# Waiting block by block in the dense down projection, and other places for two small pieces of work

## The reference

```python
x = x + 0.5 * L0_ffn(norm(x))   # stage 1, dense:   down(silu(gate) * up), 384 hidden
x = x + L0_attn(norm(x))        # stage 2, mixing:  a recurrence over time (WKV)
x = x + 0.5 * L0_ffn(norm(x))   # stage 3, dense:   same weights as stage 1
x = x + 0.5 * L1_ffn(norm(x))   # stage 4, experts: 8 experts, the best 2 per token
x = x + L1_attn(norm(x))        # stage 5, flow attention
x = x + 0.5 * L1_ffn(norm(x))   # stage 6, experts: same weights as stage 4
```

```python
gate = einsum('bsd,hd->bsh', x, w_gate / 127)
up   = einsum('bsd,hd->bsh', x, w_up / 127)
out  = einsum('bsh,dh->bsd', silu(gate) * up, w_down / 127)
```

## Time and profile before

| | |
|---|---|
| median of three runs | 1009.28 us |
| the profiled execution | 1007.76 us |
| its span (first to last instruction) | 1006.0 us |
| PE busy | 859.9 us (85%) |
| DVE busy | 711.1 us (71%) |
| ACT busy | 638.6 us (63%) |
| POOL busy | 604.4 us (60%) |
| mean granted clock of TensorE | 0.947 |

### The profile page before, as it was taken

How to read it: one execution, slowest core, us unless ns; L and a number is a source line. 1 busy time by engine, 2 the same in 40 slices (tenths; PEclk the granted TensorE clock), 3 DMA queues, 4 the chain that set the end, 5 groups by cost and what they waited for, 6 DMA issues and landing times.

```text
span 1006.0 us, 14102 instructions
## 1 busy us (share of the span) xinstructions
PE 859.9 (85%) x3862; PEld 460.3 (46%) x3862; DVE 711.1 (71%) x1535; ACT 638.6 (63%) x1153; POOL 604.4 (60%) x610
## 2 busy tenths in 40 slices
PE   7879677767975999999996688888886899999997
PEld 6734333354432444444443355555543344444443
DVE  6945469965563878887863277777786787887774
ACT  3167489967755887778783444444322787778884
POOL 2064675667458766666675254444457766667674
PEclk9999788869997999999997799999997999999999
DMA  8000000000002222211120000000000213223320
GB/s 213 11 1 0 0 0 1 1 1 1 1 0 85 84 86 85 79 48 58 69 84 0 1 1 0 1 1 1 1 1 1 101 69 95 94 94 95 94 95 22
DMA packets 27406, 42.10 MB, mean 42 GB/s; under 512 B 5320, under 2 KB 19036, under 8 KB 27356
## 3 DMA queue, kind: packets, MB, share of 16 engines
q1 hardware_dynamic: 27356, 41.52, 13.0%
HBM read 39.15 MB, written 2.36 MB: 41 GB/s over the span
## 4 chain that ended last, share of the span: by engine, by line
PE 35%; issue 22%; DVE 19%; POOL 14%; ACT 9%; SPq 1%; DVEq 0%; POOLq 0%; DMA 0%; ACTq 0%
PE bank L1478 7%; PE bank L1480 7%; PE bank L1479 7%; POOL arena L810 5%; POOL arena L754 4%; PE bank L1708 3%; DVE arena L1324 3%; ACT bank L1001 3%; POOL rstd L712 2%; DVE arena L1367 1%; DVE arena L1366 1%; DVE stats L1173 1%; PE bank L1678 1%; ACT arena L993 1%; PE bank L1715 1%
## 5 line engine op out<-in xcount | busy, mean ns | idle before, releaser
L790 POOL TENSOR_TENSOR arena<-arena 128x512 f16<-128x512 f32 x256 | 295.3, 1166 | 125.3 <-ACT arena L993 123.5
L1324 DVE TENSOR_TENSOR arena<-bank,arena 128x512 f32<-128x512 f32 x256 | 172.5, 685 | 79.6 <-ACT bank L1001 63.3
L993 ACT ACTIVATE arena<-arena 128x512 f16<-128x512 f32 x256 | 160.8, 628 | 73.8 <-DVE arena L1324 73.7
L1001 ACT ACTIVATE bank<-bank,eb 128x512 f32<-128x512 f32 x256 | 166.8, 656 | 18.9 <-PE bank L1480 18.5
L817 POOL TENSOR_TENSOR arena<-arena 128x512 f32<-128x512 f32 (+1 forms) x24 | 32.7, 1371 | 117.2 <-DVE arena L1442 89.9
L1478 PE MATMUL bank<-arena,ew1hi 128*128 128x512 f16 x256 | 98.5, 385 | 2.0 <-DVE arena L1324 2.0
L1479 PE MATMUL bank<-arena,ew1hi 128*128 128x512 f16 x256 | 98.5, 385 | 0.0
L1480 PE MATMUL bank<-arena,ew1lo 128*128 128x512 f16 x256 | 97.9, 382 | 0.0
L1478 PE MATMUL bank<-arena,ew2hi 128*128 128x512 f16 x256 | 97.3, 380 | 0.1
L1479 PE MATMUL bank<-arena,ew2hi 128*128 128x512 f16 x256 | 97.3, 380 | 0.0
L1480 PE MATMUL bank<-arena,ew2lo 128*128 128x512 f16 x256 | 97.3, 380 | 0.0
(11 more groups left out here) (274 smaller groups left out, 1876.2 us busy)
## 6 DMA issues: line engine op xcount, KB each, us to landing
arena<-wrows SPq DMA_DIRECT2D x64, 512.0 KB, 5.4
X<-in_L_attn_x_dram SPq DMA_DIRECT2D x8, 256.0 KB, 4.3
out_dram<-X SPq DMA_DIRECT2D x8, 256.0 KB, 6.7
arena<-in_L_ffn_ew_dram SPq DMA_DIRECT2D x2, 512.0 KB, 6.4
arena<-in_L_ffn_ew_dram SPq DMA_DIRECT2D x1, 1024.0 KB
wrows<-arena SPq DMA_DIRECT2D x16, 16.0 KB
arena<-in_L_ffn_gens_dram SPq DMA_DIRECT2D x1, 192.0 KB, 2.7
arena<-in_L_ffn_w_gate_dram SPq DMA_DIRECT2D x1, 192.0 KB, 2.9
```

The costliest lines, as they stand in the source:

```text
L790: pool.tensor_tensor(mo.hlo[:, u % 8, :], mo.hw[:, u % 4, :], mo.hhi[:, u % 8, :], ALU.subtract).then_inc(S.hlo, 1)
L993: A(mo.hhi[:, u % 8, :], mo.hw[:, u % 4, :], ACT.Copy).then_inc(S.hhi, 1)
L1001: A(bank[MM1_BANK[u]][:, :], bank[MM1_BANK[u]][:, :], ACT.Gelu, scale=1.0 / WS, bias=eb1[:, u:u + 1]).then_inc(S.gelu, 1)
L1324: TT(mo.hw[:, u % 4, :], bank[MM1_BANK[u]][:, :], mo.wB[:, p, u // EB, :], ALU.mult)\
```

## The change

There are three parts.

1. Down projection. In both dense stages PE no longer waits for the remainders of all three blocks ahead of the nine products. It waits for block 0 ahead of the first three, for block 1 ahead of the next three, and for block 2 ahead of the last.
2. Last chunk of both dense stages. ACT rounds block 1 before the silu of block 2 instead of after it. The remainder of block 2 is no longer POOL's but DVE's: it stands behind DVE's addition of chunk 6 to x and ahead of that chunk's statistics.
3. Small products. They leave `fold_a` and become `fold_small`, which PE does in the first chunk of stage 1, between gate and up of block 1 and the transposes of the second chunk. DVE's `fold_a` moves with them to the first chunk of stage 1. `FOLD.stage` becomes 1, and POOL's `low_fold` is pinned to stage 3, where it was.

```diff
--- before.py
+++ after.py
@@ -502,7 +502,7 @@
 
 
         FOLD = Buffers()
-        FOLD.m, FOLD.turn, FOLD.small, FOLD.out, FOLD.stage = 0, (1, 2, 3, 4), 6, (1, 2), 3
+        FOLD.m, FOLD.turn, FOLD.small, FOLD.out, FOLD.stage = 0, (1, 2, 3, 4), 6, (1, 2), 1
 
         CREDIT = 1
 
@@ -748,14 +748,14 @@
 
                 def step(i, p, lead, mid, lag):
                     if mid:
-                        for j in range(HB):
+                        for j in range(HB if lead else HB - 1):
                             u = HB * p + j
                             pool.wait_ge(S.hhi, HB * i + j + 1)
                             pool.tensor_tensor(f0.hlo[:, u, :], f0.h[:, u % 2, :], f0.hhi[:, u, :],
                                                ALU.subtract).then_inc(S.hlo, 1)
-                        if number == FOLD.stage and not lag:
+                        if number == 3 and not lag:
                             low_fold((0, 1))
-                        if number == FOLD.stage and not lead:
+                        if number == 3 and not lead:
                             low_fold((2, 3))
                 pipeline(pool, first, NCH, step, led=number == 1)
 
@@ -923,13 +923,15 @@
                         if lead and mid and j == HB - 1:
                             act.wait_ge(S.tr, i + 2)
                             A(f0.xhi[:, 1 - p, :], bank[0][:, :], ACT.Copy).then_inc(S.xhi, 1)
+                        if mid and not lead and j > 1:
+                            low(j - 1)
                         if mid:
                             act.wait_ge(S.gu, HB * i + j + 1)
                             A(f0.sg[:, (HB * p + j) % 2, :], bank[1 + (HB * p + j) % 2][:, :], ACT.Silu,
                               scale=QSCALE).then_inc(S.sg, 1)
                         if lead and mid and j == 0:
                             normalise(i + 1, 1 - p, S.z, first, number)
-                        if mid and j:
+                        if mid and j and (lead or j == 1):
                             low(j - 1)
                         if lag and j == 1:
                             act.wait_ge(S.down_mm, i)
@@ -1241,7 +1243,14 @@
                             .then_inc(S.xlo, 1)
                     if lag:
                         dve.wait_ge(S.down, i)
-                        finish_x(i - 1, first, bank[7][:, :], 0.5 * QSCALE, S.x, i + CREDIT)
+                        add_to_x(i - 1, first, bank[7][:, :], 0.5 * QSCALE, S.x)
+                        if mid and not lead:
+                            u = HB * p + HB - 1
+                            dve.wait_ge(S.hhi, HB * i + HB)
+                            dve.wait_ge(S.hlo, HB * i + HB - 1)
+                            TT(f0.hlo[:, u, :], f0.h[:, u % 2, :], f0.hhi[:, u, :], ALU.subtract).then_inc(S.hlo, 1)
+                        wait_apart(dve, S.x, i + CREDIT)
+                        tile_stats(i - 1 - first)
                 pipeline(dve, first, NCH, step, led=number == 1)
 
             def mixing(S, first, number):
@@ -1518,7 +1527,6 @@
 
             def fold_a():
 
-                small = bank[FOLD.small]
                 pe.wait_ge(S0.w_moe, 16 * N_MOE)
                 tr(bank[FOLD.m][:, 0:E], sm.eb2, ident[0:E, 0:E]).then_inc(S0.small, 1)
                 pe.wait_ge(S0.w_ew2, 32)
@@ -1533,6 +1541,11 @@
                     if g == 1:
                         pe.wait_ge(S0.mt, 1)
                         mm(bank[FOLD.m][:, 0:P], sm.MT, rot(2), start=True, stop=True).then_inc(S0.mtp, 1)
+
+            def fold_small():
+
+                small = bank[FOLD.small]
+                pe.wait_ge(S0.w_moe, 16 * N_MOE)
                 pe.wait_ge(S0.folds, 2)
                 mm(small[:, 0:E], ones[:, :], gate_b[:, :], start=True, stop=False, skip_group_check=True)
                 mm(small[:, 0:E], beta_all[:, :], gate_w[:, :], start=False, stop=True, skip_group_check=True)
@@ -1575,13 +1588,15 @@
                                              f0.xlo[:, p, :])
                             last.then_inc(S.gu, 1)
                         if lag and j == 1:
-                            pe.wait_ge(S.hlo, HB * i)
                             for m in range(HB):
+                                pe.wait_ge(S.hlo, HB * i + m + 1 - HB)
                                 u = HB * (1 - p) + m
                                 w = slice(m * P, (m + 1) * P)
                                 last = three(bank[5][:, :], f0hi[:, 2, w], f0lo[:, 2, w], f0.hhi[:, u, :],
                                              f0.hlo[:, u, :], start=(m == 0), stop=(m == HB - 1))
                             last.then_inc(S.down_mm, 1)
+                        if number == FOLD.stage and mid and not lag and j == 1:
+                            fold_small()
                         if lead and j == 1:
                             turn_chunk(Z, 1 - p, S.z, i + 2, S.tr)
                     if lag:
```

## The result

| | before | after |
|---|---|---|
| median, range (4 runs each) | 1009.79 us (1007.32 to 1010.81) | 994.88 us (992.09 to 996.10) |
| span of the profiled execution | 1006.0 us | 993.6 us |
| mean granted clock of TensorE | 0.947 | 0.944 |

The ratio is 0.9854, 95% interval 0.9837 to 0.9871: 14.7 us faster, between 13.0 and 16.5. The forecast was 995.7. Lines of the changed program stand a few numbers later: `three` is L1487 to L1489 (was L1478 to L1480), the transposes of Z L1574, those of y L1607, the output projection L1628, the one-column products L1554, the copy of the down projection L938, the new remainder on DVE L1251.

What follows compares the result with a forecast made beforehand. In steady dense chunks, a circle through POOL's remainders and PE's down projection set the 7.41 us step. Terms -9.5 - 3.0 + 1.3 - 1.2 - 1.2 = -13.6 on the 1009.28 median gave 995.7 us; whole range 991.5 to 1002.

Steps and rivals of the forecast that it cites:

- the likeliest case: The forecast itself for the whole kernel, all parts of the change at their predicted sizes: 995.7 us, chance 0.64.
- A: Split wait in 14 steady dense chunks: PE's 0.70 us gap before the down projection goes; -9.5 us, bounds 0 and -9.5.
- B: End of mixing: without the small products, the output projection and fold start earlier; -3.0 us, bounds -2.0 and -3.6.
- C: First chunk of stage 1: the small products there delay block 2 at half clock; +1.3 us, +3 if the clock recovers later.
- D: Last chunk of stage 1: PE's products end earlier, but POOL's bias rows limit the gain; -1.2 us, bounds -0.4 and -2.6.
- E: Last chunk of stage 3: statistics and variance end earlier, the variance clear of POOL's L731; -1.2 us, bounds -0.5 and -1.6.
- The slower rival: Both dense stages: PE without pauses is granted a lower clock; 1019 us at clock 0.8; chance 0.05.

Runs made afterwards that it cites:

- experiments 1 and 2: 1: the kernel before with only the block-by-block wait, 1000.5 us. 2: the changed kernel with one wait for all three remainders again, 1004.5 us.
- no split: The changed kernel with one wait for all three remainders before the down projection again; 1004.5 us.
- Experiment 5: The changed kernel with the 17 one-column products of stage 1 widened to 128 equal columns, one of them used; 994.1 us.
- Experiment 7: The changed kernel without POOL's splitting of the flow attention's biases, which the output then lacks; 993.8 us.
- ACT's order only: The changed kernel with ACT's early rounding of block 1 kept, but POOL making the last remainder and DVE's statistics not waiting; 995.3 us.
- Experiments 4 and 8: Both on the changed kernel. 4: old last chunk, split wait kept, 996.8 us. 8: ACT's early rounding kept, last remainder back on POOL, 995.3 us.
- pause and wide: The changed kernel with the small products moved to PE's pause in mixing, ahead of the fold's first half, and widened to 128 columns; 992.2 us.
- all three: The changed kernel with small products in PE's mixing pause, widened to 128 columns, and POOL making stage 1's third remainder; 993.6 us.
- experiments 7 and 9: Both on the changed kernel. 7: without POOL's bias splitting, 993.8 us. 9: small products in PE's mixing pause and 128 columns wide, 992.2 us.

## Why the prediction was right

The forecast was 995.7, the measured time 994.9, and the likeliest case came in. The time changed by 14.7 where the sum said 13.6, the spans of the two profiled executions by 12.4. In that one pair the terms add up to -13.1 (A -9.6, B -1.9, C +1.1, D -1.0, E -1.7), and the setup was 0.5 longer. By steps:

- **A, the split wait: -9.5 forecast, -9.6 measured.** 0.70 in twelve steps, and 0.58 and 0.63 in the two first ones (First 14.12 to 13.54; in stage 3 from the first silu to the y transposes 11.38 to 10.75). (The forecast's own pieces, 12 x 0.70 and 2 x 0.6, make 9.6, not 9.5.) That ACT's slack of 0.68 is just used up and does not bind was the risk; the row of L938 shows no idle time and the step equals PE's work. Shown by experiments 1 and 2.
- **B, products out of mixing: -3.0 forecast, about -2.9 measured, -1.9 in the one pair of traces.** The mean of Turn is 16.2 in the three kernels with the products there and 13.3 in the seven that have them in stage 1. These are single executions, and the new place spreads by 1.8, the old one by 2.8. The place was right, and so was the warning that ACT's copies wait for PE again. In the one pair ACT's first normalising of stage 3 comes 3.2 closer to the last exponential (231.45 and 224.06), as forecast; 1.3 of that is lost behind it, where the first products of stage 3 run at 0.50 (1.00 before). The prediction looked for the lower clock in the fold alone, at 1.1.
- **C, products in stage 1: +1.3 forecast, +1.1 to +2.8 measured** (First 14.68 to 16.33 against 13.54; no split 15.45 against 14.12; 1.8 in the mean of six). +3 stood in the prediction as the case of a clock that takes longer to come back, and two executions came near it. The row, busy 1.00 at clock 0.50, decided this rightly. The Trainium skill (TensorE: Matmul & The Clock Gate, The HAM clock gate) lets the clock depend on how busy PE has been; read as the trace's busy share this would have made C 0, and here PE was busy 2.00 of 2.00 us when the clock went to 0.62 and then 0.50. Experiment 5 shows that C was all clock: 0 with wide products.
- **D, last chunk of stage 1: -1.2 forecast, -0.9 measured, for another reason.** That the number came near is luck. What limits it was right. Counted from the y transposes of the last steady chunk (109.01; 105.82), PE's transposes ahead of mixing come 2.7 earlier (forecast 2.6), the variance 0.2 later (0.4 to 0.5) and POOL's first product of mixing 1.0 later (0.5), since L692 took 0.89 longer. Experiment 7 shows that the bias rows were a limit. Wrong was the cause of the gain. The split wait alone gives -1.4 (Mix 119.96 and 119.74 against 121.92, less the 0.70 of A), and DVE's remainder in front of the statistics takes about 0.5 back (Mix 119.97 to 120.59 in four executions with it, mean 120.33; 119.47 with ACT's order only). The two groups nearly touch, so the 0.5 is an estimate from single executions. The step that failed: "PE's last three products end near 112.7, 2.8 earlier than before" is measured against one wait for all blocks. Without the split that holds in part: in the no-split kernel the transposes ahead of mixing come 0.6 earlier against their stage, and Mix is 0.67 shorter. But that wait went with A: in the split-only kernel the transposes ahead of mixing already come 2.4 of the 2.7 earlier (104.30 to 112.92).
- **E, last chunk of stage 3: -1.2 forecast, -1.7 measured.** The term was mis-sized in its last part: from the end of L1251 to the end of the variance I allowed up to 2.4, and it took 1.84 (284.24 to 286.08). The Trainium skill (SBUF — State Buffer, Who interferes with whom) says that the issue order decides which of the two blocks. I had read from it only that L1251 could be the one that stands, at a price of 0.7. In the trace L1251 started at 283.54 and took 0.70, as in stage 1 (0.69), and POOL's pair took 2.72 instead of 2.26. A window that begins behind the first of the pair shows the second by itself, started 0.11 after L1251:

```profile
283.65 1.60 POOL L731 TENSOR_TENSOR ew2lo<-arena,ew2hi 128x512 f16<-128x512 f32 x1
```

  The two met, and POOL, the later one, stood. The trace agrees with the page. Experiments 4 and 8 show that E hangs on POOL being rid of a remainder.

The slower rival (a lower clock without pauses) is out: the steady chunks ran at 6.70 throughout, and the mean clock is 0.944 against 0.947.

## What to carry to other kernels

When one wait covers several blocks, check whether only the last products need the last block: waiting block by block gave two thirds of this change and all of what a new order in the last chunk of stage 1 seemed to give. When two edits meet in one place, work out the second on top of the first, not on the kernel before. Work moved into a pause is not free when the products are one column wide: read the granted clock beside them, and try the same products wider.

## What the runs showed of the hardware

- Narrow float32 products and the clock: 32 passes of one column took 4.67 us and the clock went from 1.00 to 0.50 during them; 32 passes of 128 columns in the same place took 3.84 at 1.00 throughout. In PE's pause of mixing the narrow stream took 6.99 (0.50 to the end) and the wide one 6.63 and 5.53 (pause and wide, all three), 0.50 at first and 1.00 at the end. Which of their properties the chip goes by was not tried.
- Where the clock stands at the end of mixing moves identical code by up to 2.8 us (Turn 14.67, 16.40 and 17.43 with the products in the old place). It falls in PE's pauses and in the narrow stream, and what comes earlier or later shifts which piece of work finds it low; gains of 0.8 to 1.4 us were given back in this way (experiments 7 and 9, B in the one pair). Where a stage begins behind a pause, one pair of traces doesn't settle a term under 2 us.
- POOL's L692 took 1.26 in the kernel before and 2.06 to 2.15 in the seven with the split wait that were looked at (1.27 in no split): the bias rows ahead of mixing lengthened by 0.8 to 0.9 once POOL's and DVE's work met at other times.
- One pair of instructions, DVE's product and POOL's of the first chunk of mixing, met in both kernels, and each time the one that started later was the longer. Before, DVE first:

```profile
140.82 0.66 DVE L1295 TENSOR_TENSOR arena<-arena 128x512 f32<-128x512 f32 x1
140.97 1.46 POOL L773 TENSOR_TENSOR arena<-arena 128x512 f32<-128x512 f32 x1 [1.16 <-DVE arena L1292]
```

  After, POOL first:

```profile
137.67 1.57 DVE L1304 TENSOR_TENSOR arena<-arena 128x512 f32<-128x512 f32 x1 [3.69 <-POOL arena L771]
137.61 1.08 POOL L773 TENSOR_TENSOR arena<-arena 128x512 f32<-128x512 f32 x1
```
